# Planes of the score matmuls stored once and fetched by 16-row loads, with every hand-written order of work redrawn

## The reference

```python
# L0, per image: ll is the low band, high the three others
q, k = l2norm(q), l2norm(k)                      # 8 heads of 16 channels, 1024 positions
attn = einsum('bhnd,bhmd->bhnm', q, k) * 16 ** -0.5
attn = where(attn among the 512 largest of its row, attn, -1e9)
out  = softmax(attn) @ v                         # then 1x1 projection, group norm
high = high + alpha * gn(conv1x1(silu(gn(dwconv3x3(high)))))
x    = x + 0.1 * iwt(ll + out, high)
x    = x + 0.1 * gn(conv1x1(gelu(gn(conv1x1(x)))))
# L1: q, k have 16 channels, 4096 positions
attn = softmax((Wq x + bq)^T (Wk x + bk) / 4)
x    = gamma * (Wo ((Wv x + bv) attn^T) + bo) + x
```

## Time and profile before

| | us |
|---|---|
| median of 3 runs (5665.16 to 5668.21) | 5667.28 |
| span of the profiled execution | 5667.7 |
| heads of image 0 alone, one slot | about 47.7 |
| merged slot (seven times eight) | about 63.8 |
| boundary, from the end of the heads to the first `maxima` | about 121.6 |
| chunk of image 7 alone | about 44.0 |

### The profile page before, as it was taken

One profiled execution on the slowest core, in us unless ns is written; L12 is line 12 of the kernel. 1 busy time (PEld: TensorE's weight loads), 2 busy tenths in 40 slices (PEclk: granted clock), 3 DMA queues, 4 the chain that ended last, 5 costly groups with the idle time before them and its releaser, 6 DMA issues.

```text
span 5667.7 us, 92692 instructions
## 1 busy us (share of the span) xinstructions
PE 4766.2 (84%) x30180; PEld 3123.3 (55%) x30180; DVE 4618.9 (81%) x9087; ACT 4256.4 (75%) x6779; POOL 250.6 (4%) x125
## 2 busy tenths in 40 slices
PE   4444899988999889988999889998899889997799
PEld 2001366654666456663666546664466636664588
DVE  4887799987999789986999879997799879996553
ACT  3883699948998499966999489884899669994333
POOL 2001000010000200010000100002000100000000
PEclk7555799998999989998999989999899989998899
DMA  1001200012001110012000120011100120001100
GB/s 68 7 11 50 74 15 16 15 56 76 16 20 43 59 43 18 16 61 74 15 15 13 58 76 16 20 43 50 51 16 18 59 75 15 15 13 43 36 12 16
DMA packets 104805, 199.97 MB, mean 35 GB/s; under 512 B 36632, under 2 KB 41656, under 8 KB 100184
## 3 DMA queue, kind: packets, MB, share of 16 engines
q1 hardware_dynamic: 104280, 193.56, 11.1%
HBM read 110.61 MB, written 82.05 MB: 34 GB/s over the span
## 4 chain that ended last, share of the span: by engine, by line
PE 41%; DVE 23%; ACT 15%; issue 14%; SPq 3%; DMA 3%; DVEq 0%; ACTq 0%; POOL 0%; POOLq 0%
PE PS L582 16%; ACT work L1183 7%; PE PS L548 5%; DVE M L1760 4%; DVE MX L1928 4%; PE PS L566 4%; ACT work L1243 3%; DVE work L1751 3%; PE PS L514 3%; PE PS L524 3%; DVE work L1743 2%; PE PS L1057 2%; ACT arena L1175 2%; DVE arena L1857 2%; DMA work<-TPT 1%
## 5 line engine op out<-in xcount | busy, mean ns | idle before, releaser
L582 PEld LDWEIGHTS PS<-V,work 128*128 128x128 f32 x16384 | 2106.7, 193 | 155.8 <-issue 7.0
L582 PE MATMUL PS<-V,work 128*128 128x129 f32 x16384 | 2125.2, 277 | 2.5 <-ACT work L1243 1.2
L1183 ACT ACTIVATE work<-arena,T 128x1024 bf16<-128x1024 f32 x1504 | 1725.8, 1150 | 22.7 <-DVE T L1671 18.8
L1928 DVE TENSOR_REDUCE MX<-PS 128x1 f32<-128x512 f32 x2048 | 1399.3, 687 | 249.6 <-PE PS L548 233.9
L1243 ACT ACTIVATE work<-PS 128x1024 f32<-128x1024 f32 x1024 | 1046.8, 1024 | 334.0 <-PE PS L566 332.3
L548 PE MATMUL PS<-KP,QP 96*128 96x512 bf16 x2048 | 845.5, 414 | 137.3 <-DVE MX L1928 95.3
L566 PE MATMUL PS<-QP,KP 99*128 99x512 bf16 x2048 | 624.6, 387 | 77.5 <-ACT work L1243 54.2
L1175 ACT ACTIVATE arena<-PS 128x1024 f32<-128x1024 f32 x512 | 523.2, 1022 | 216.7 <-PE PS L446 209.5
L1857 DVE SCALAR_TENSOR_TENSOR arena<-PS,work 128x512 f32<-128x512 f32 x896 | 606.2, 684 | 67.3 <-ACT work L1235 65.3
L1760 DVE MAX8 M<-work 128x8 f32<-128x512 f32 x1024 | 648.4, 682 | 1.0
L1235 ACT ACTIVATE work<-PS 128x512 f32<-128x512 f32 x896 | 530.8, 601 | 119.9 <-PE PS L514 116.1
(11 more groups left out here) (193 smaller groups left out, 4160.8 us busy)
## 6 DMA issues: line engine op xcount, KB each, us to landing
scr<-work SPq DMA_DIRECT2D x96, 256.0 KB
work<-scr SPq DMA_DIRECT2D x128, 192.0 KB, 2.8
work<-in_x SPq DMA_DIRECT2D x16, 1024.0 KB, 7.7
arena<-in_x SPq DMA_DIRECT2D x8, 2048.0 KB, 9.9
scrX<-arena SPq DMA_DIRECT2D x8, 2048.0 KB, 14.2
XR<-scrX SPq DMA_DIRECT2D x64, 256.0 KB, 2.8
out<-YO SPq DMA_DIRECT2D x64, 256.0 KB, 2.0
scrL<-work SPq DMA_DIRECT2D x24, 512.0 KB, 2.6
```

The lines of the kernel that those rows point to most:

```text
L582: last = mm(PS[:, 5 + i // 2, 136 * (i % 2):136 * (i % 2) + 129], P1[:, (16 * j + k) % 3, t, 128 * i:128 * i + 128], V1[:, mt, :], start=( ...
L1183: A(junk[:, m % 2, :], scores(h, i), ACT.Sign, scale=-1.0, bias=T[:, h % 2, i:i + 1], accum_out=CA[:, h % 2, i:i + 1]).then_inc(s["ca"], 1)
L1928: V.reduce_max(MX[:, c % 2, i, w:w + 1], PS[:, maxbank(c, k, l0), :], AX.X).then_inc(s["mr"], 1)
```

## The change

- `TERMS` is put in another order: (0,0), (0,1), (0,2), (1,0), (1,1), (2,0). The same six products are summed.
- L0 planes: `scr0` holds each plane once; three stores of 512 KB (rows of 4 KB) replace twelve of 256 KB. A head is loaded with twelve DMAs of 16 rows of 2 KB in the place of two of 96 rows. Head 0 is loaded as soon as planes 0 and 1 have landed; its two pieces of plane 2 come straight from the SBUF tile (`head0_late`). Heads 1 and 2 are loaded after the L1 planes.
- L1 planes: each plane is stored by four DMAs as soon as it is made (rows of 2 KB into rows of 8 KB), and loaded by twelve DMAs of 16 rows of 8 KB, keys first; the loads of planes 0 and 1 don't wait for plane 2.
- All hand-written lists (merged slots of PE, ACT and DVE, `alone`, `between`, `closing`) are drawn anew. The same calls stand in them; `chunks` (L1 alone) is as before.

```diff
+            def load_head(h, parts=(0, 1, 2)):
+                for j, pair in enumerate(TERMS):
+                    for w, t in enumerate(pair):
+                        if t in parts:
+                            sp.dma_start(QK0[HD * j:HD * j + HD, h % 3, w, :], scr0[t, d, w, :]).then_inc(done, 16)
+            def load_planes(parts):
+                for w, dst in ((1, KP1), (0, QP1)):
+                    for j, pair in enumerate(TERMS):
+                        if pair[w] in parts:
+                            sp.dma_start(dst[HD * j:HD * j + HD], scr1[pair[w], HD * w:HD * w + HD, :]).then_inc(s["qp1"], 16)
+            def store_plane(n, t, made):
+                sp.wait_ge(s[made], (n + 1) * 2)
+                sp.dma_start(scr0[t].rearrange("p w n -> p (w n)"), PT[:, t, :]).then_inc(s["scrw"], 16)
...
             def between(f, n, fin, opn):      # SP
...
-                    store_planes(n, 0, "p0")
-                    store_planes(n, 1, "p1")
-                    store_planes(n, 2, "p2")
+                    store_plane(n, 0, "p0")
+                    store_plane(n, 1, "p1")
                     sp.wait_ge(s["vt"], (n + 1) * 2)
                     sp.sem_inc(s["free"], 1)
-                    sp.wait_ge(s["scrw"], (n + 1) * 192)
-                    for h in range(3):
+                    sp.wait_ge(s["scrw"], n * 48 + 32)
+                    load_head(0, (0, 1))
+                    store_plane(n, 2, "p2")
+                    head0_late()
+                if fin:
+                    for a, made in enumerate(("p10", "p11", "p12")):
+                        sp.wait_ge(s[made], f + 1)
+                        for j in range(4):
+                            sp.dma_start(scr1[a][:, N0 * j:N0 * j + N0], PT1[32 * j:32 * j + 32, a, :])
+                    sp.wait_ge(s["scrw1"], (f + 1) * 128)
+                    load_planes((0, 1))
+                    sp.wait_ge(s["scry1"], (f + 1) * 64)
+                    load_planes((2,))
+                if opn:
+                    sp.wait_ge(s["scrw"], (n + 1) * 48)
+                    for h in range(1, 3):
                         load_head(h)
```

The turn from one merged slot to the next, on PE and DVE:

```diff
 PE
-                    maxrow(h)
-                    last_weigh(h, 7)
                     l1_weigh(h - 1, 15, (0,))
+                    last_weigh(h, 7)
                     l1_weigh(h - 1, 15, (1,))
-                    weigh(h - 1, 3); weigh(h - 1, 4); weigh(h - 1, 5)
+                    maxrow(h)
+                    weigh(h - 1, 3)
                     score(h + 1, 0)
+                    weigh(h - 1, 4)
                     l1_turn(h - 1)
-                    l1_score(h, 0)
+                    weigh(h - 1, 5)
+                    score(h + 1, 1)
                     weigh(h - 1, 6)
                     maxima(h + 1, 0)
-                    score(h + 1, 1)
+                    l1_score(h, 0)
                     weigh(h - 1, 7)
 DVE
                     eight(h, 0)
+                    half_m(h - 1, 6, 1)
+                    eight(h, 1)
                     half_m(h - 1, 7, 0)
-                    apart(h, 2)
                     half_m(h - 1, 7, 1)
                     l1_norm(h - 1)
                     excess(h, 1)
-                    eight(h, 1)
+                    apart(h, 2)
+                    apart(h, 3)
                     l1_out(h - 1)
...
                     maxima(h + 1, 2)
+                    centre(h + 1, 0)
+                    apart(h, 4)
                     apart(h, 5)
                     maxima(h + 1, 3)
-                    centre(h + 1, 0)
```

More of the change, by code:

```diff
@@ L654, in search @@
-                    l1_weigh(h - 1, 2, (0,))
+                    l1_weigh(h - 1, 2, (1,))
+                    l1_score(h - 1, 4)
                     maxima(h, 7)
-                    l1_weigh(h - 1, 2, (1,))
+                    l1_weigh(h - 1, 3, (0,))
+                    maxima(h, 8)
                     score(h, 7)
-                    l1_score(h - 1, 4)
-                    maxima(h, 8)
-                    maxima(h, 9)
-                    l1_weigh(h - 1, 3, (0,))
-                    maxima(h, 10)
@@ L669, in search @@
                     l1_score(h - 1, 7)
-                    l1_weigh(h - 1, 5, (0,))
-                    maxima(h, 12)
-                    l1_weigh(h - 1, 5, (1,))
-                    l1_score(h - 1, 8)
+                    l1_weigh(h - 1, 6, (1,))
+                    l1_weigh(h - 1, 7, (0,))
                     found_sum(h - 1)
                     maxima(h, 13)
-                    l1_weigh(h - 1, 6, (0,))
+                    l1_weigh(h - 1, 7, (1,))
+                    l1_score(h - 1, 8)
@@ L677, in search @@
+                    maxima(h, 14)
+                    turn(h - 1)
                     l1_score(h - 1, 9)
-                    maxima(h, 14)
-                    l1_weigh(h - 1, 6, (1,))
-                    l1_weigh(h - 1, 7, (0,))
-                    turn(h - 1)
                     maxima(h, 15)
-                    l1_weigh(h - 1, 7, (1,))
+                    l1_weigh(h - 1, 8, (0,))
                     maxima(h, 16)
-                    l1_weigh(h - 1, 8, (0,))
+                    l1_weigh(h - 1, 8, (1,))
@@ L720, in search @@
+                    half_t(h - 1, 4, 1)
                     half_t(h - 1, 5, 0)
                     l1_score(h - 1, 13)
-                    maxima(h, 28)
+                    maxima(h, 29)
+                    l1_weigh(h - 1, 12, (0,))
+                    weigh(h - 1, 2)
+                    maxima(h, 30)
                     half_t(h - 1, 5, 1)
-                    l1_weigh(h - 1, 12, (0,))
-                    maxima(h, 29)
+                    l1_score(h - 1, 14)
                     l1_weigh(h - 1, 12, (1,))
+                    maxima(h, 31)
@@ L763, in closing @@
                     l1_weigh(NH - 1, 6, (1,))
+                    found_sum(NH - 1)
                     l1_score(NH - 1, 8)
+                    l1_weigh(NH - 1, 7, (0,))
+                    turn(NH - 1)
                     l1_score(NH - 1, 9)
-                    l1_weigh(NH - 1, 7, (0,))
-                    found_sum(NH - 1)
                     l1_weigh(NH - 1, 7, (1,))
                     l1_weigh(NH - 1, 8, (0,))
-                    turn(NH - 1)
+                    l1_score(NH - 1, 10)
@@ new lines, in closing @@
+                    l1_weigh(NH - 1, 11, (1,))
+                    l1_weigh(NH - 1, 12, (0,))
+                    half_t(NH - 1, 4, 0)
+                    half_t(NH - 1, 4, 1)
+                    l1_score(NH - 1, 14)
+                    l1_weigh(NH - 1, 12, (1,))
+                    l1_weigh(NH - 1, 13, (0,))
+                    half_t(NH - 1, 5, 0)
+                    weigh(NH - 1, 1)
+                    l1_score(NH - 1, 15)
+                    l1_weigh(NH - 1, 13, (1,))
+                    half_t(NH - 1, 5, 1)
```

622 lines of the change are left out of this document (295 added, 327 removed).

## The result

The changed kernel takes 5598.8 us (median; 5597.2 to 5605.3) where the kernel before, on the same chip, takes 5666.2: a ratio of 0.9885, 95% interval 0.9873 to 0.9896. It is 67 us faster; the forecast was 5630, 38 us faster. The time lies inside the range of 5580 to 5690 and outside the forecast's own band of 5610 to 5650. The profiled execution has a span of 5596.3 us, 71.4 less than before.

A forecast was written before the change was run, and what follows sets the result against it. Merged slots, three engines above 92% busy, bind as a loop: DVE to the threshold, then ACT. Boundaries -8, slots -25, image 0 -4, last boundary -0.5 make -38 us from 5667.7: forecast 5630, range 5580 to 5690.

The forecast's parts named there:

- L0 planes: At the boundary between images: storing each plane once lets head 0's score come 0.7 us sooner; bounds 0 and 1.25 us.
- L1 planes: At the boundary: loads start 1.2 us later, stay at 107 GB/s, maxima start sooner; 1.2 us gained a boundary, 8 in seven.
- rival D: At the boundaries: wide rows load at 218 GB/s, then `values1` binds; 4 us more, 7 at the last, 5619; chance 0.09.
- The upper bound of 2.5 us a boundary: At the boundary: most that the second attention's plane loads could gain, bounds 0 and 2.5 us.
- Slots: In 49 merged slots: reordered calls give -0.5 us each, -25 us; ends -73 and +25 us.
- the -0.62 on DVE for `eight` and `apart`: Merged slot, last `half_m` to threshold: `eight(h, 1)` leaves, `apart(h, 2)` enters, -0.62 us of DVE work.
- The -0.13 for ACT's half: Merged slot, `turned` to last `half_e`: one `count` leaves, one `l1_exp` enters, -0.13 us on ACT.
- Image 0: Image 0 alone: counts ahead of the first mask fill DVE's wait; 0.6 us in each of seven slots, -4; bounds +5, -15.
- `closing`: In the closing stretch of each image: the same calls, so nothing, +-1 us in seven.
- Rival A: In the merged slots: ACT's idle time does count, -1.2 us a slot, 5596 in all; chance 0.20.
- `scrL`: At the boundary: bands stored later behind more loads; `apart(0, 0)` hidden by 5 us at best, 3 us late at worst.
- C: In the merged slots: `maxrow` moved later, rows land late for `l1_score(h, 0)`, PE stands; slower, 5700; chance 0.19.

## Why the prediction was right, and where it wasn't

**L0 planes.** Three issues instead of twelve, as said. "The first score has no wait for DMA" failed: PE waits 1.55 us for the late pieces, where it waited 1.25 for the loads. The 0.7 us that I took were not there; the lower bound, nothing, was the value, and the planes alone gave nothing (1.0000).

**L1 planes.** That 8 KB rows keep 107 GB/s was right (106), and rival D is out. Wrong is the start: I wrote that "the loads of planes 0 and 1 no longer wait for plane 2" and put it 1.2 us later than before; it is 3.5 us later in image 1 and 2.0 on average. They don't wait for plane 2 to land, but they stand behind its four stores in SP's queue, and SP waits there for `p12`. I had read the wait on `scrw1` and passed over the one on `p12` above it. On DVE `part1(2)` stands behind `centre0(0)`, which waits for the fourth eviction. The kernels with `part1(2)` moved show the order that counts: stores first, in one piece.

Two numbers of this part were off in themselves. The upper bound of 2.5 us a boundary doesn't follow from its own terms: with the last `values1` at 1336.4 no start of the loads could give more than 1.8, as rival D has it. And the 218 GB/s of the stores is high: 3.15 MB in 13.92 us of issue would be 226, while the transfers themselves ran at some 200 to 206 GB/s in the same stretch. Neither changes which term binds.

**Slots.** -32 us for -25: near in size, wrong in its ledger, so the nearness is in part luck. The slot has the 63.2 us of the forecast, but ACT's wait is 2.2 us and not below 1, and the -0.62 on DVE for `eight` and `apart` measured 0.14 at most. DVE is busy on both sides of the last `half_m`, so an operation moved across that mark only moves the mark. What has to be counted is the work between the two marks at which another engine is waited for: DVE's up to the threshold, 32.6 to 31.1 us, and ACT's from `turned` on, 28.5 to 29.4. The -0.13 for ACT's half was +0.9. The halves came out at -1.6 and +1.3 in this slot; in the typical slot of image 1 (63.8 to 63.2) that leaves 0.5 to 0.6 us, the forecast's size. The total passes it by the last two slots of each image (-20 us), less what the first one loses (+5). Which single move frees DVE's first half is not settled.

**Image 0.** -6.3 for -4, but not where I put it. I had taken 0.6 us off each slot; from the first threshold to the eighth the seven slots take 337.2 us where they took 333.6, 0.5 us more each. All of the gain lies behind the last threshold, 48.5 to 39.0 us, in the same operations on the bands as in the closing: beside POOL they took 6.8 us more than alone before and 3.5 now, and DVE has less of them left there.

**`closing`, "the same calls: nothing, +-1 us in seven"**, is the step that failed, at 29 us. That the calls are the same is no argument: DVE stood still 12 of 66 us there, and I had not opened a window on it. Behind the 29 us lie a larger gain and two losses: the list is worth 8.7 us a closing where POOL is idle, POOL's presence takes 5 of them, and the late `based` goes with 2 us at the next turn of the loop, of which 0.9 is left in the boundary's length.

**Rival A** has the nearest time, 5596, and not by its reasons: it wanted 1.2 us from every slot, and they gave 0.66; the closing's 29 us, which it had at nothing as well, fill the hole. That the two sums meet is luck.

**`scrL`.** `apart(0, 0)` runs without a wait for the bands' store, as forecast. C, the row maxima's copy late for `l1_score(h, 0)`, doesn't show in the slot's waits.

The Trainium skill, "SBUF — State Buffer", section "Door 1: The DMA port swizzle", held where it mattered: with 16 partitions the loads stayed at 106 GB/s with either size of row, and 64 partitions moved the same bytes in less of the engines' time. The section gives a rate by ports and doesn't speak of the size of a row; that rows of 8 KB load no faster is what the runs show. The ports alone didn't set the time of the wider loads, as told above.

## To carry to other kernels

Cut both traces at marks that a queue issues anyway, and open a window on every stretch before you cost it at nothing; an engine's idle time there is what a new order can win. Moving work across a point only counts if another engine waits at that point. Don't add up parts that were measured alone: here they made 27 of 67 us. And look at what a moved operation runs beside: here the largest gain, 40 us, was a wait added to an engine that had nothing urgent to do.

## What the hardware showed that I had not expected

DVE's operations on two SBUF operands (128x1024, f32) took 1.22 us alone and 1.45 to 3.85 beside POOL's on SBUF, and POOL's 3.7 to 3.8 instead of 2.8; DVE's `half_m`, which has one operand in PSUM, stayed at 0.67 to 0.69. The Trainium skill, "SBUF — State Buffer", section "Who interferes with whom", has the mechanism: the two engines share a pair of ports that one of them holds for its whole instruction. The times agree: 1.45 to 3.85 us is an operation of 1.22 behind what is left of one of POOL's 2.8.

A load of 0.9 MB issued 3 to 4 us before `OX`, at the turn of the loop, went with 3.4 to 4.9 us to PE's first instruction in 21 of 25 turns of five kernels; with the load 9 to 14 us before it was 2.1 to 3.4 in 43 of 45 turns of the nine others. The trace also records the transfers that bring instructions. In all 70 turns PE's first instruction came 1.5 to 2.0 us after the last of them on queue q8 (16 KB) had landed. It landed 0.8 us after `OX` in the median with the early load and 2.4 with the late one; and in the four turns with a late load in which it landed within 1 us, PE started after 2.1 to 2.7. An interval as steady as that says that PE waits for its instructions there, and with the late load they come 1.5 us later. That the load itself is in their way, on the same DMA engines, is my reading: no run moved the load alone.

And four stores queued behind ten loads into 16 partitions took 7 us to land.
